# Two of three blocks of the experts' activations turned by DMA, and the down product two tiles behind the up product

## The reference, cut to what matters

```python
h1 = jnp.einsum('td,edh->eth', X, W1)                      # 512 -> 352
h3 = jnp.einsum('td,edh->eth', X, W3)
y = jnp.einsum('eth,ehd->etd', jax.nn.silu(h1) * h3, W2)   # 352 -> 512
out = jnp.einsum('etd,te->td', y, gate_full)               # two gates per token are not zero
```

## Time and profile before

| | us |
|---|---|
| median of three runs | 1217.57 |
| the profiled execution | 1217.89 |
| its span on the core | 1216.1 |
| PE busy in the span | 1189.8 |
| DVE busy | 805.9 |
| POOL busy | 506.3 |
| ACT busy | 417.7 |

### The profile page before, as it was taken

How to read it: one execution, slowest core, us unless ns; L and a number is a source line. 1 busy time by engine, 2 the same in 40 slices (tenths; PEclk the granted TensorE clock), 3 DMA queues, 4 the chain that set the end, 5 groups by cost and what they waited for, 6 DMA issues and landing times.

```text
span 1216.1 us, 25326 instructions
## 1 busy us (share of the span) xinstructions
PE 1189.8 (98%) x9054; PEld 776.8 (64%) x9054; DVE 805.9 (66%) x1578; ACT 417.7 (34%) x873; POOL 506.3 (42%) x409
## 2 busy tenths in 40 slices
PE   7999999999999999999999999999999999999996
PEld 2646666666666666767777777656666666666663
DVE  5647778878776777655857754266666666666665
ACT  4424444445443432333323323222222222222221
POOL 2212566656564554222112112345445554455543
PEclk9999999999999999999999999999999999999998
DMA  7816597998788978745434535579787897779783
GB/s 238 228 40 168 125 250 192 214 234 212 182 222 185 229 209 197 173 99 120 122 87 104 137 85 117 111 150 135 132 141 140 131 132 139 138 135 136 133 127 45
DMA packets 253255, 185.27 MB, mean 152 GB/s; under 512 B 186496, under 2 KB 198784, under 8 KB 253132
## 3 DMA queue, kind: packets, MB, share of 16 engines
q1 hardware_dynamic: 217368, 114.40, 42.1%
q0 software_dynamic: 20512, 45.62, 22.4%
q10 hardware_dynamic: 15256, 23.62, 6.7%
HBM read 87.07 MB, written 52.75 MB: 115 GB/s over the span
## 4 chain that ended last, share of the span: by engine, by line
PE 90%; DVE 2%; issue 2%; DMA 2%; POOL 1%; ACT 1%; SPq 0%; ACTq 0%; POOLq 0%; DVEq 0%
PE ps_o L87 7%; PE ps_o L89 7%; PE ps_o L88 7%; PE ps_vs L87 6%; PE ps_vs L88 6%; PE ps_vs L89 6%; PE ps_kh L87 4%; PE ps_vh L87 4%; PE ps_vh L88 4%; PE ps_vh L89 4%; PE ps_kh L88 4%; PE ps_kh L89 4%; PE ps_qh L87 4%; PE ps_qh L89 4%; PE ps_qh L88 4%
## 5 line engine op out<-in xcount | busy, mean ns | idle before, releaser
L444 POOL DMA_INDIRECT out<-y,slot_row x71 | 139.3, 1963 | 190.3 <-DVE y L882 138.7
L89 PE MATMUL ps_o<-w_all,xt 128*128 x568 | 177.5, 313 | 0.0
L88 PE MATMUL ps_o<-w_all,xt 128*128 x568 | 177.5, 313 | 0.0
L87 PE MATMUL ps_o<-w_all,xt 128*128 x568 | 177.5, 312 | 0.0
L874 DVE SCALAR_TENSOR_TENSOR gate_row<-gate_rows,batch_weight,gate_row 128x512 f32<-128x512 f32 x213 | 158.9, 746 | 2.5
L368 POOL DMA_INDIRECT out<-s_sum,row_no x32 | 53.8, 1680 | 197.6 <-DVE s_sum L623 192.0
L1133 ACT ACTIVATE at<-ps_y 128x384 f16<-128x384 f32 x71 | 34.8, 491 | 250.7 <-PE ps_y L1353 247.1
L330 POOL TENSOR_TENSOR h<-cen,rows_f 128x512 f32<-128x512 f32 x32 | 40.6, 1270 | 130.6 <-ACT cen L901 115.4
L89 PE MATMUL ps_qh<-ht,wqkv 128*128 128x128 f16 x512 | 87.4, 219 | 0.0
L88 PE MATMUL ps_qh<-ht,wqkv 128*128 128x128 f16 x512 | 87.4, 219 | 0.0
L87 PE MATMUL ps_qh<-ht,wqkv 128*128 128x128 f16 x512 | 87.4, 219 | 0.0
(11 more groups left out here) (251 smaller groups left out, 3341.2 us busy)
## 6 DMA issues: line engine op xcount, KB each, us to landing
w_stage<-in_w_d ACTq DMA_DIRECT2D x64, 176.0 KB
xb<-in_x SPq DMA_DIRECT2D x32, 256.0 KB, 3.7
xr<-in_x SPq DMA_DIRECT2D x32, 256.0 KB, 4.0
out<-x SPq DMA_DIRECT2D x32, 256.0 KB, 3.6
h_d<-hl SPq DMA_DIRECT2D x32, 256.0 KB, 2.5
h2t_d<-h2t SPq DMA_DIRECT2D x32, 256.0 KB, 3.5
s_ht<-h2t_d SPq DMA_DIRECT2D x32, 256.0 KB, 3.6
sstage<-in_sh_flat SPq DMA_DIRECT2D x32, 136.0 KB, 3.6
```

Source lines behind the costliest of these rows:

```text
L87: nc.tensor.matmul(out, lh, rh, start=first, stop=False, skip_group_check=True)
L88: nc.tensor.matmul(out, lh, rl, start=False, stop=False, skip_group_check=True)
L89: return nc.tensor.matmul(out, ll, rh, start=False, stop=last, skip_group_check=True)
L444: pool.indirect_dma_start(m.out, bass.IndirectOffsetOnAxis(ap=m.slot_row[:, t:t + 1], axis=0), m.y[:, t % Y_RING, :], None, compute_op=ALU ...
```

## The change

Of the three 128-column blocks of `a`, the first two (`DMA_TURNED`) are no longer turned by PE. ACT copies them as rows into the high half of `a_rows` (`e_high_rows`), DVE subtracts for the low half (`e_low_rows`), and SP turns these 512 columns with one DMA transpose into `at_d`, a ring of 3. PE turns only the third block, into `at_p`. The last tile (`LAST`) is still turned whole by PE. On SP, the new transposes stand between the old ones: the activations of tile t, then `turn_g(t + 6)`. On PE, the down product follows the up product at a distance of two tiles: `e_up(t)`, then `e_down(t - 2)`. The gate rows and `y` move back by one tile with it. POOL's program is unchanged. The second and third group of `wmod` loads share one semaphore each, and `modulate(j)` for j of 2 or more waits for all four loads of its group.

The core of the diff:

```diff
+AT_RING, DMA_TURNED = 3, 2
 # sync_program
-    for t in range(4, SLOT_TILES):
+    for t in range(4, G_RING):
         turn_g(t)
+    for t in range(LAST):
+        if t == 0:
+            sp.wait_ge(m.s_t1_done, 2 * CHUNKS)
+        sp.wait_ge(m.a_lo, t + 1)
+        at_least(sp, m.ey_done, t - AT_RING + 1)
+        sp.dma_start_transpose(m.at_d[t % AT_RING][:, :, :], m.a_rows[:, t % 2, :, :].rearrange("p s n -> p (s n)")).then_inc(m.at_loaded[t % AT_RING], 16)
+        if t + G_RING < SLOT_TILES:
+            turn_g(t + G_RING)
 # vector_program
+    def e_low_rows(t):
+        if t < LAST:
+            v.wait_ge(m.a_hi, t + 1)
+            v.tensor_tensor(m.a_rows[:, t % 2, 1, :], m.a[:, t % 2, 0:DMA_TURNED * P], m.a_rows[:, t % 2, 0, :], ALU.subtract).then_inc(m.a_lo, 1)
...
-        v.tensor_tensor(m.at[:, t % 2, 1, :, :], m.ps_a[:, :, :], m.at[:, t % 2, 0, :, :], ALU.subtract).then_inc(m.e_at_lo, 1)
+        v.tensor_tensor(m.at_p[t % AT_RING][:, 1, :], m.ps_a[:, DMA_TURNED, :], m.at_p[t % AT_RING][:, 0, :], ALU.subtract).then_inc(m.e_at_lo, 1)
...
-    for t in range(1, SLOT_TILES + 1):
-        e_low(t - 1)
-        gate_rows_of(t - 1, 1)
-        gate_rows_of(t - 1, 2)
+    for t in range(1, SLOT_TILES + 2):
+        if t <= SLOT_TILES:
+            e_low(t - 1)
+        if t >= 2:
+            gate_rows_of(t - 2, 1)
+            gate_rows_of(t - 2, 2)
         if t < SLOT_TILES:
             e_multiply(t)
-        gate_rows_of(t - 1, 3)
-        e_out(t - 1)
+        if t >= 2:
+            gate_rows_of(t - 2, 3)
+        if t < SLOT_TILES:
+            e_low_rows(t)
+        if t >= 2:
+            e_out(t - 2)
 # scalar_program
+    def e_high_rows(t):
+        if t < LAST:
+            act.wait_ge(m.e_act, t + 1)
...
+            if t >= 2:
+                act.wait_ge(m.at_loaded[(t - 2) % AT_RING], ring_use(t - 2, AT_RING))
+            act.activation(m.a_rows[:, t % 2, 0, :], m.a[:, t % 2, 0:DMA_TURNED * P], ACT.Copy).then_inc(m.a_hi, 1)
 # tensor_program
-        for k in range(IT):
+        for k in range(DMA_TURNED if t < LAST else 0, IT):
             mm = nc.tensor.transpose(m.ps_a[:, k, :], m.a[:, t % 2, k * P:(k + 1) * P], m.ident[:, :])
...
     def e_down(t, expert):
-        pe.wait_ge(m.e_at_lo, t + 1)
         at_least(pe, m.ey_ready, t)
+        if t < LAST:
+            pe.wait_ge(m.at_loaded[t % AT_RING], ring_use(t, AT_RING))
...
     for t in range(1, SLOT_TILES):
...
         e_turn(t - 1)
-        e_up(t, following)
+        e_up(t, experts[t])
...
-        e_down(t - 1, expert)
+        if t >= 2:
+            e_down(t - 2, experts[t - 2])
+    e_turn(LAST)
+    e_down(LAST - 1, experts[LAST - 1])
+    e_down(LAST, experts[LAST])
```

More of the change, by code:

```diff
@@ L27 @@
 SLOTS = SLOT_TILES * P
+LAST = SLOT_TILES - 1
 SCALE = 64.0
@@ L865, in e_multiply @@
                                op0=ALU.mult, op1=ALU.mult).then_inc(m.e_act, 1)
+    def e_low_rows(t):
+        if t < LAST:
+            v.wait_ge(m.a_hi, t + 1)
+            v.tensor_tensor(m.a_rows[:, t % 2, 1, :], m.a[:, t % 2, 0:DMA_TURNED * P], m.a_rows[:, t % 2, 0, :], ALU.subtract).then_inc(m.a_lo, 1)
     def e_low(t):
-        v.wait_ge(m.e_at_hi, t + 1)
-        v.tensor_tensor(m.at[:, t % 2, 1, :, :], m.ps_a[:, :, :], m.at[:, t % 2, 0, :, :], ALU.subtract).then_inc(m.e_at_lo, 1)
+        v.wait_ge(m.e_at_hi, t + 1 if t < LAST else t + 2)
+        v.tensor_tensor(m.at_p[t % AT_RING][:, 1, :], m.ps_a[:, DMA_TURNED, :], m.at_p[t % AT_RING][:, 0, :], ALU.subtract).then_inc(m.e_at_lo, 1)
+        if t == LAST:
+            v.tensor_tensor(m.at_d[t % AT_RING][:, 2:4, :], m.ps_a[:, 0:2, :], m.at_d[t % AT_RING][:, 0:2, :], ALU.subtract).then_inc(m.e_at_lo, 1)
     def gate_rows_of(t, b):
@@ L884, in vector_program @@
     e_multiply(0)
+    e_low_rows(0)
     add(CHUNKS - 1)
-    for t in range(1, SLOT_TILES + 1):
-        e_low(t - 1)
-        gate_rows_of(t - 1, 1)
-        gate_rows_of(t - 1, 2)
+    for t in range(1, SLOT_TILES + 2):
[4 more added lines that the diff above has]
+            gate_rows_of(t - 2, 2)
         if t < SLOT_TILES:
             e_multiply(t)
-        gate_rows_of(t - 1, 3)
-        e_out(t - 1)
+        if t >= 2:
[4 more added lines that the diff above has]
+            e_out(t - 2)
 def scalar_program(nc, m, act):
@@ L1074, in scalar_program @@
                 cols = slice((2 + 2 * s) * C, (4 + 2 * s) * C)
-                act.dma_start(m.wmod[:, k, cols], m.wmod_d[k * P:(k + 1) * P, cols]).then_inc(m.wmod_loaded[KC * (s + 1) + k], 16)
+                act.dma_start(m.wmod[:, k, cols], m.wmod_d[k * P:(k + 1) * P, cols]).then_inc(m.wmod_loaded[KC + s], 16)
         if s < TILES:
@@ L1125, in e_silu @@
         at_least(act, m.at_done, t - 1)
+        at_least(act, m.a_lo, t - 1)
         act.activation(m.a[:, t % 2, 0:INTER], m.ps_h1[:, 0:INTER], ACT.Silu, scale=1.0 / SCALE).then_inc(m.e_silu, 1)
+    def e_high_rows(t):
+        if t < LAST:
+            act.wait_ge(m.e_act, t + 1)
+            if t == 0:
+                act.wait_ge(m.at_lo, EARLY_STEPS)
+            if t >= 2:
+                act.wait_ge(m.at_loaded[(t - 2) % AT_RING], ring_use(t - 2, AT_RING))
+            act.activation(m.a_rows[:, t % 2, 0, :], m.a[:, t % 2, 0:DMA_TURNED * P], ACT.Copy).then_inc(m.a_hi, 1)
     def e_high(t):
@@ L1131, in e_high @@
             act.wait_ge(m.s_t1_done, 2 * CHUNKS)
-        at_least(act, m.ey_done, t - 1)
-        act.activation(m.at[:, t % 2, 0, :, :], m.ps_a[:, :, :], ACT.Copy).then_inc(m.e_at_hi, 1)
+        at_least(act, m.ey_done, t - AT_RING + 1)
+        act.activation(m.at_p[t % AT_RING][:, 0, :], m.ps_a[:, DMA_TURNED, :], ACT.Copy).then_inc(m.e_at_hi, 1)
+        if t == LAST:
+            act.activation(m.at_d[t % AT_RING][:, 0:2, :], m.ps_a[:, 0:2, :], ACT.Copy).then_inc(m.e_at_hi, 1)
     def first_gate_row(t):
@@ L1141, in scalar_program @@
     e_silu(0)
-    first_gate_row(0)
+    e_high_rows(0)
     for t in range(1, SLOT_TILES):
         e_high(t - 1)
-        first_gate_row(t)
+        first_gate_row(t - 1)
         e_silu(t)
-    e_high(SLOT_TILES - 1)
+        e_high_rows(t)
+    e_high(LAST)
+    first_gate_row(LAST)
 def tensor_program(nc, m, pe):
@@ L1236, in modulate @@
         for k in range(KC):
-            pe.wait_ge(m.wmod_loaded[KC * (j // 2) + k], 16)
+            if j < 2:
+                pe.wait_ge(m.wmod_loaded[k], 16)
+            else:
+                pe.wait_ge(m.wmod_loaded[KC + j // 2 - 1], 16 * KC)
             mm = nc.tensor.matmul(m.ps_mod[j], m.sct[:, k, :], m.wmod[:, k, j * C:(j + 1) * C], start=k == 0, stop=k == KC - 1)
@@ L1356, in e_down @@
     def e_down(t, expert):
-        pe.wait_ge(m.e_at_lo, t + 1)
         at_least(pe, m.ey_ready, t)
+        if t < LAST:
+            pe.wait_ge(m.at_loaded[t % AT_RING], ring_use(t, AT_RING))
         for k in range(IT):
             w = min(P, INTER - k * P)
-            mm = split_matmul(nc, m.ps_ey[:, 0:C], (m.at[0:w, t % 2, 0, k, :], m.at[0:w, t % 2, 1, k, :]),
+            if k < DMA_TURNED:
+                turned = (m.at_d[t % AT_RING][:, k, :], m.at_d[t % AT_RING][:, DMA_TURNED + k, :])
+            else:
+                turned = (m.at_p[t % AT_RING][0:w, 0, :], m.at_p[t % AT_RING][0:w, 1, :])
+            if k == 0 and t == LAST:
+                pe.wait_ge(m.e_at_lo, t + 2)
+            if k == DMA_TURNED and t < LAST:
+                pe.wait_ge(m.e_at_lo, t + 1)
+            mm = split_matmul(nc, m.ps_ey[:, 0:C], turned,
                               (m.w2[0:w, bass.ds(expert, 1), k, 0, :].rearrange("p o n -> p (o n)"),
@@ L1368, in tensor_program @@
     pe.wait_ge(m.consts, CONSTS)
-    expert = expert_of(0)
-    e_up(0, expert)
+    experts = [expert_of(0)]
+    e_up(0, experts[0])
     down(CHUNKS - 1)
@@ L1373, in tensor_program @@
     for t in range(1, SLOT_TILES):
-        following = expert_of(t)
+        experts.append(expert_of(t))
         e_turn(t - 1)
-        e_up(t, following)
-        if t == 1:
+        e_up(t, experts[t])
+        if t == 2:
             pe.wait_ge(m.s_t1_done, 2 * CHUNKS)
-        e_down(t - 1, expert)
-        expert = following
-    e_turn(SLOT_TILES - 1)
-    e_down(SLOT_TILES - 1, expert)
+        if t >= 2:
[3 more added lines that the diff above has]
+    e_down(LAST, experts[LAST])
 def place_buffers(nc, m):
@@ L1536, in place_buffers @@
     m.passed = sb("passed", [1, SLOT_TILES, E], F32)
-    GATE_AT, ACT_AT, AT_AT, UP_BYTES = SHARED_AT + 8192, SHARED_AT + 12288, SHARED_AT + 14336, UP_COLS * 2
+    GATE_AT, ACT_AT, AT_AT, T1_AT, UP_BYTES = SHARED_AT + 8192, SHARED_AT + 12288, SHARED_AT + 14336, SHARED_AT + 24576, UP_COLS * 2
     staged, third, second = region(W_STAGE_AT, W_AT), region(SHARED_AT, SHARED_AT + 4096), region(SHARED_AT + 4096, SHARED_AT + 8192)
@@ L1546, in place_buffers @@
     m.a = sb("a", [P, 2, IT * P], F32)
-    m.at = region(GATE_AT, ACT_AT)("at", [P, 2, 2, IT, P], F16)
```

(7 more changed lines are left out.)

## The result

The changed kernel takes 1408.07 us (median of four runs, 1406.25 to 1409.83), 1.156 times the time before (95% interval 1.154 to 1.159), 190.5 us more. The forecast was 1365 us with a range of 1280 to 1425. One run of one experiment (TensorE kept busy, 1388.79 us) fell in a slower state of the chip and is left out of its median.

A forecast was written before the change was run, and what follows sets the result against it. TensorE's work bounds the kernel at 5.853 us a tile; the change adds a circle through SP's queue. 32 turns of 15.42 + 0.85 us take 520.6 against 374.6: with the smaller terms +147.6 on 1217.9, 1365 us, range 1280 to 1425.

The forecast's parts named there:

- One turn: Down product to down product two tiles on: 15.42 us plus 0.85 for the clock, against 11.26 us of TensorE work.
- scatter to gather: On POOL, from the scatter's start to the gather's start: 2.27 us of each turn.
- gather to SP's transpose: From the gather's start to SP's transpose of those rows: 5.28 us, given as the mean of all 64.
- landing and semaphore, to the down product: New transpose from issue to landing 2.8 us (ends 1.8 and 3.7), then semaphore to TensorE 0.14 us.
- The circle: Down product, `y`, scatter, gather, transpose of gathered rows, transpose of activations, down product two tiles on; TensorE waits 4.2 us per turn.
- The clock's term: TensorE's clock falls after its wait: 0 to 1.7 us lost per turn, the middle 0.85 taken.
- the second rival: Cold in every turn: one wait of 4.2 us, the whole 1.7 us clock loss, turn 17.12 us, 1393 us; chance 21%.
- The 195.4 us in the earlier trace: SP's queue waits for gathers before the change: 44 pieces, read as 4.44 us of every tile.
- the 2.9 us at the end: DVE has one more tile's three gate steps and one `y` before the last `y`: +2.9 us.
- the first rival: Short circle: quicker gathers, scatters and landing, the clock holds; turn 13.14 us, 1265 us; chance 18%.
- the third: Long circle: new transposes contend with gathers and scatters; landing 3.7, turn 18.57 us, 1439 us; chance 13%.
- The fourth rival: The circle doesn't bind because the gather has landed when SP comes to it; TensorE stays the bound, 1205 us; chance 5%.

The follow-up runs named there:

- TensorE kept busy: The changed kernel with 8 more matmuls of 512 columns, which nobody reads, in front of each down product: 1374.77 us, 1.126 times the time before.
- the last experiment: The changed kernel, with POOL holding both the scatter of tile t and the gather behind it until the activations of tile t+1 have landed: 1576.69 us, 1.294.
- the run with the lag alone: The changed kernel with down product, gate rows, scatter and gather one tile later, but all three blocks turned by TensorE as before: 1218.34 us, 1.0005.
- the run with t+4: The changed kernel, but on SP the activations of tile t are followed by the transpose of gathered rows t+4 instead of t+6: 1204.51 us, 0.988.
- the run with half the bytes: The changed kernel with a DMA transpose of 256 columns of activations in place of 512, the output lacking the low half's part: 1398.13 us, 1.147.
- the run with t+5: The changed kernel, but on SP the activations of tile t are followed by the transpose of gathered rows t+5 instead of t+6: 1238.98 us, 1.018.

## Why the prediction was right, and where its sum was off

The mechanism is as predicted, point by point: the waits stand before the first matmul into `ps_vs` and are released by a DMA into `at_d`; each transpose into `at_d` follows one into `xt` by 1.3 us; TensorE is busy for 76% (some 70% forecast); the clock is below 1.00. The turns of even and odd tiles didn't share the wait: it came mostly in one piece every two tiles, as the waits of 34 pieces for 64 tiles say.

The time of 1408 lies 43 us above the forecast. One turn, as forecast, as the mean of the 64 turns from tile 0 to tile 65 in the changed kernel's timelines, and as the mean of the 34 of them whose last down product waits for its activations:

| term | forecast | 64 turns | 34 that end in a wait |
|---|---|---|---|
| down product to `y`, with the clock's loss | 2.14 + 0.85 | 2.69 | 3.17 |
| `y` | 0.69 | 0.69 | 0.69 |
| to the scatter | 0.86 | 0.82 | 0.83 |
| scatter to gather | 2.27 | 1.88 | 1.88 |
| gather to SP's transpose | 5.28 | 4.60 | 4.36 |
| SP's transpose to the new one | 1.24 | 1.36 | 1.35 |
| landing and semaphore, to the down product | 2.8 + 0.14 | 5.43 | 5.06 |
| turn | 16.27 | 17.48 | 17.35 |

(The terms add up to the turn but for rounding.) In the other 30 turns the activations had landed before TensorE came to them, so their last term is TensorE's work on the neighbour tile and tells nothing of the landing. The circle's own terms are those of the last column.

The term that was mis-sized is the landing of the new transpose: I took 2.8 us from the rows of larger ones, less half of their issue. That is near its time alone (2.5 in the last experiment), but on the chain it shows 4.73 and 4.65, and with the semaphore it takes 5.06 on the mean. My range for it ended at 3.7, since I had the contention with POOL's transfers in a rival and not in the term. The circles of even and odd tiles stand about one tile apart, so the activations that TensorE waits for are issued while the scatter of the neighbour tile is in flight: in 33 of the 34 turns it began 0.3 to 3.7 us before, and scatters land 4.5 to 6.1 us after they begin. This is 2.1 us a turn, 68 us over 32 turns. Quicker gathers and scatters gave back 1.3 us a turn, 42 us. What remains, with 0.2 for the clock and 0.1 for SP, is 1.1 us a turn, 35 us; the mean of all 64 turns is 1.21 us over the forecast, 39 us, nearly all of the difference of 43.

So two errors of opposite sign partly cancelled, and that the time fell into the range is in part luck: with gathers and scatters as forecast it would have been some 1450 us, above the 1425. The clock's term is partly luck too. I took the middle of 0 and 1.7 us because the wait might split into two of 2.1; it came in one piece, which was the second rival's condition for the whole 1.7. It cost about 1.0 (3.17 less 2.14), because 8 of the 34 down products that had waited ran at full speed and most others were slowed in part.

Three smaller readings were off and move little. The 195.4 us in the earlier trace rows are 4.44 us a piece but 3.5 us a tile: 44 of the 56 transposes in that stretch waited. The mean of all 64 gathers to SP's transpose in the kernel before is 5.35 us; 5.28 leaves out the longest, 9.22. And the 2.9 us at the end don't show in the run with the lag alone.

Gathers were shorter than in the kernel before, as the first rival had it, and the landing was longer, as the third had it: both rivals with another length of the circle were right in one term each. That gathers were shorter because the stage was slower fits the DMA share (0.60 against 0.79), but no run tests it. The fourth rival's 1205 us, what the change would have been without the circle, is what the run with t+4 measured (1204.51).

## What to carry to other kernels

When a transfer joins an issue queue, read what the entries in front of it wait for, and follow these waits back: if they reach the consumer of an earlier transfer of the same kind, the latency of the whole ring becomes the pace, and a wait that cost nothing becomes the bound. One turn's latency divided by the tiles that it spans tells how far ahead the prefetch must stand, with a margin, since the turn grows when the pace rises (17.5 us over two tiles, 19.2 over three here); moving the prefetch by two tiles turned 15.6% slower into 1.2% faster. A latency taken from a quiet or differently timed part of a trace needs the transfers that will run beside it in the new order. And the terms of a circle are to be read where it binds: a mean over rounds that wait and rounds that don't hid half of the clock's loss here.

## What the runs showed of the hardware that was not expected

- The issue of a DMA transpose held SP for about the same time whatever its width: 1.24 us in the median for 1024 columns, 1.23 for 512 in the change (the first line below) and 1.20 for 256 in the run with half the bytes (the second). In the run with t+5 it was 1.59 for 512 columns (the third), so something other than the width moves it; what, is not shown.

```profile
L317 SPq DMA_TRANSPOSE at_d<-a_rows x70: 1189/1232/2461, 796.8 to 1385.6; - x70
L317 SPq DMA_TRANSPOSE at_d<-a_rows x70: 1167/1202/2225, 795.9 to 1379.0; - x70
L318 SPq DMA_TRANSPOSE at_d<-a_rows x70: 1189/1590/2374, 791.0 to 1212.3; - x70
```

- A share of the DMA engines of 0.99 did not slow TensorE at all in the run with t+4.
- 122 us of matmuls that compute nothing made a kernel some 33 us faster; the granted clock in the stage was 0.98 with them and 0.89 without.
